# A language-model block with routed experts on one core: first list and third choice moved between a scan and its rotations

## What is computed

```python
h = W.T[x] + b + positions                        # embedding
u = layernorm(h)
Bu = einsum('blh,ph->blp', u, B_bar)              # state-space layer, 64 complex states
xs = associative_scan(x[t] = Lambda_bar * x[t-1] + Bu[t])
h = h + gelu(2 * Re(einsum('blp,hp->blh', xs, C)) + D * u)
x = layernorm(h)
top 2 of 8 experts by logits x @ router_w.T + router_b, weights softmax of the two
out = h + sum over the two: weight * (fc2_e @ (silu(h1) * h2) + fc2_b),  (h1, h2) = fc1_e @ x + fc1_b
```

## Time and profile before

| | us |
|---|---|
| runs (three) | 192.73, 191.54, 193.65 |
| median | 192.73 |
| profiled execution, its own time | 190.8 |
| its span, first to last instruction | 189.0 |
| mean granted TensorE clock | 0.818 of full |
| busy: TensorE, VectorE, ScalarE, GpSimd | 132.8, 112.4, 77.3, 91.0 |
| fourth scan on VectorE starts | 69.70 |
| third scatter on GpSimd, first issue | 77.05 |
| fourth scatter on GpSimd, first issue | 95.47 |

### The profile page before, as it was taken

How to read it: one execution, slowest core, us unless ns; L and a number is a source line. 1 busy time by engine, 2 the same in 40 slices (tenths; PEclk the granted TensorE clock), 3 DMA queues, 4 the chain that set the end, 5 groups by cost and what they waited for, 6 DMA issues and landing times.

```text
span 189.0 us, 3503 instructions
## 1 busy us (share of the span) xinstructions
PE 132.8 (70%) x805; PEld 105.0 (56%) x805; DVE 112.4 (59%) x472; ACT 77.3 (41%) x245; POOL 91.0 (48%) x113
## 2 busy tenths in 40 slices
PE   0273169998869879751991269999996979867910
PEld 0021116758559458541981169988886978765300
DVE  4975159599894896840660027755665665542484
ACT  2223216145182152842542065656555656554000
POOL 5777850000574674573267634645554645446200
PEclk9998555897885975996589559999999999999555
DMA  4222147050151431422133113332310100100297
GB/s 137 69 57 56 47 120 168 3 164 3 27 215 42 129 113 43 101 68 70 45 89 85 55 29 98 102 87 72 100 34 32 36 22 28 42 28 27 75 363 230
DMA packets 15093, 15.65 MB, mean 83 GB/s; under 512 B 2995, under 2 KB 11701, under 8 KB 15074
## 3 DMA queue, kind: packets, MB, share of 16 engines
q1 hardware_dynamic: 10914, 9.39, 18.5%
q0 software_dynamic: 2784, 5.28, 8.8%
q10 hardware_dynamic: 1376, 0.77, 1.3%
HBM read 9.62 MB, written 6.27 MB: 84 GB/s over the span
## 4 chain that ended last, share of the span: by engine, by line
PE 48%; DVE 24%; another core or an unknown queue 10%; issue 9%; ACT 6%; DMA 1%; DVEq 0%; ACTq 0%
PE bank L1238 9%; PE bank L1214 8%; PE bank L1224 8%; PE bank L1204 8%; PE bank L1056 7%; PE bank L1258 3%; DVE stats L626 2%; DVE res L841 1%; DVE zst L613 1%; PE bank L1030 1%; DVE res L624 1%; ACT xT L957 1%; ACT ysb L986 1%; ACT w1b L932 1%
## 5 line engine op out<-in xcount | busy, mean ns | idle before, releaser
L355 POOL DMA_INDIRECT sorted_rows<-rows,slot x32 | 32.2, 1005 | 42.4 <-DVE slot L656 33.8
L753 DVE SCALAR_TENSOR_TENSOR act_h<-bank,w1b,sil 128x128 f32<-128x128 f32 x78 | 23.6, 344 | 33.7 <-ACT sil L966 20.9
L1238 PE MATMUL bank<-w_sb,act_h 128*128 x156 | 26.9, 296 | 11.9 <-ACT ysb L986 10.1
L366 POOL DMA_INDIRECT results<-ysb,dest x22 | 21.7, 985 | 18.3 <-ACT ysb L986 11.6
L1238 PEld LDWEIGHTS bank<-w_sb,act_h 128*128 128x128 f32 x156 | 21.5, 200 | 14.3 <-issue 13.8
L1224 PE MATMUL bank<-xT,w1b 128*128 128x128 f32 x156 | 25.8, 292 | 5.1 <-issue 4.1
L966 ACT ACTIVATE sil<-bank,w1b 128x128 f32<-128x128 f32 x78 | 24.7, 375 | 6.1 <-PE bank L1214 4.4
L1214 PE MATMUL bank<-xT,w1b 128*128 128x128 f32 x156 | 25.7, 290 | 0.0
L366 POOL DMA_INDIRECT results<-ysb,xt x17 | 17.2, 1009 | 17.6 <-ACT ysb L986 15.3
L1224 PEld LDWEIGHTS bank<-xT,w1b 128*128 128x128 f32 x156 | 22.3, 206 | 5.5 <-issue 4.3
L957 ACT COPY xT<-bank 128x128 f32<-128x128 f32 x39 | 10.4, 268 | 33.1 <-PE bank L1204 18.5
(11 more groups left out here) (232 smaller groups left out, 200.2 us busy)
## 6 DMA issues: line engine op xcount, KB each, us to landing
w_sb<-w_all SPq DMA_DIRECT2D x8, 386.0 KB
xt<-sorted_rows SPq DMA_DIRECT2D x39, 65.0 KB, 1.8
yres<-results SPq DMA_DIRECT2D x8, 256.0 KB, 4.0
sorted_rows<-pad SPq DMA_DIRECT2D x1, 520.0 KB, 6.1
sorted_rows<-rows,slot POOLq DMA_INDIRECT x32
out<-res SPq DMA_DIRECT2D x2, 256.0 KB, 3.3
results<-ysb,dest POOLq DMA_INDIRECT x22
results<-ysb,xt POOLq DMA_INDIRECT x17
```

Source lines behind the costliest of these rows:

```text
L355: gp.indirect_dma_start(sorted_rows[:, :], bass.IndirectOffsetOnAxis(ap=slot[:, k, t:t + 1], axis=0), rows[:, k, t, :], None).then_inc(s_s ...
L366: gp.indirect_dma_start(results[:, :], bass.IndirectOffsetOnAxis(ap=target, axis=0), ysb[i][:, :], None, bounds_check=bound, oob_is_err=Fa ...
L753: v.scalar_tensor_tensor(act_h[i % 2][:, q], ps_l[sides(i)][:, q], w1b[i % 4][:, 2 * HID + 2 + c:2 * HID + 3 + c], sil[i % 2][:, q], ALU.a ...
L1238: ins = te.matmul(ps_o[sides(i)][:, 0:D], act_h[i % 2][:, c * P:(c + 1) * P], w_sb[:, bass.ds(at + W1 + c * D, D)], start=(c == 0), stop=( ...
```

## The change

Three calls change places. On VectorE `early_table(0)` and `choose(2)` go from behind `scan(3)` to its inside, behind the scan proper and ahead of the two rotations of group 3. On TensorE `positions(2)` and `count_rows(1)` go from behind the rotated products of group 3 to ahead of them. No instruction is added or removed.

```diff
@@ scan(g), VectorE @@
                 step(v.tensor_tensor_scan(zst[:, :], decay[:, :], zin[:, :], 0.0, ALU.mult, ALU.add))
+                if g == NG - 1:
+                    early_table(0)
+                    choose(2)
                 if g >= 1:
                     dve.wait_ge(s_y, 2 * g)
                 v.tensor_tensor(by_batch(zrot[:, 0, :]), by_batch(zst[:, :]), cos_b, ALU.mult).then_inc(s_zrot, 1)
@@ order on VectorE @@
             scan(3)
-            early_table(0)
-            choose(2)
             find_slots(2)
             early_counts(1)
             add_gelu(3)
@@ order on TensorE @@
             pe.wait_ge(s_rotin, NG)
             idle_products(1, ps_vs)
+            positions(2)
+            count_rows(1)
             rotated(3, 0)
             rotated(3, 1)
-            positions(2)
-            count_rows(1)
             idle_products(3, ps_vs)
             find_ends(1)
```

## The result

The changed kernel took 198.24 us (median of 4 runs, 197.99 to 199.34), the kernel before 192.72 (4 runs, 191.54 to 193.65). The ratio is 1.0301 with a 95% interval of 1.0232 to 1.0369: slower by 5.5 us, where 1.5 us less had been forecast. The profiled execution of the changed kernel took 197.99, with a span of 196.3 against 189.0.

What follows compares the result with a forecast made beforehand. TensorE was taken to bound the change's 4 us stretch and the long pause what follows. The slots' −1.58, with the first tile's 1.40 covered, rounded to −1.5: 192.73 − 1.5 = 191.2 us, range 189.6 to 195.3.

Steps and rivals of the forecast that it cites:

- What bounds, and what ends the pause: ScalarE's 6.00 us pause before copying xnT bounds what follows; it ends 1.45 us after the third scatter's last issue.
- rival a: The pause before xnT's copy has its own length whatever GpSimd does: +1.4, so 194.1 us; chance 0.12.
- an instruction fetch: Possible alternative cause of the pause before xnT: a sequencer stalls for its program block; time 194.1 us, no separate chance.
- Rival (c): The third group's earlier slots are worth nothing and both shifts drown: 192.7 us; chance 0.13.
- The rotations, +2.01: On VectorE, the third group's two rotations come 2.01 us later, behind the list and choice block of 2.10 us.
- a margin of 0.2: At the block's start on VectorE, the list's products were to be ready 0.2 us ahead, so no wait.
- The slots, 1.58 sooner: VectorE's third slots end at 74.66 instead of 76.24, so GpSimd's third scatter starts and ends 1.58 us sooner.
- Positions and count hidden: TensorE's positions and count, an estimated 0.7 us, are hidden to 0.1 behind the wait for the first rotation.
- The first tile +1.40, paid nowhere: First tile's input copy on ScalarE is 1.40 us late (2.01 − 0.61), covered by some 4 us of pause.
- rival (b): The hold on TensorE's signals catches the first tile: +1.4 to +3.8 us, 194.1 to 196.5, middle 194.7; chance 0.25.
- From xnT on everything moves along: After xnT's copy, fourth logits, choice, slots, scatter and the second pause's end all move 1.58 us sooner.
- the 0.7 us that the clock might have given back: TensorE's shorter idle time after the pause might keep its clock high: taken as 0, bounds −0.7 and +0.2.

Runs made afterwards that it cites:

- e12: VectorE half of the change alone, TensorE's order as before, against the kernel before on chip 10 (191.12): 193.09 us, ratio 1.011.
- e11: Changed kernel with SyncE's loads of tiles 3 to 8 held until the third scatter has landed, against the kernel before on chip 10 (191.12): 188.68 us, 0.9879.
- e8: Only third choice and third positions moved ahead, first list and second count left behind, against the kernel before on chip 4 (192.39): 196.31 us, ratio 1.0205.
- e7: Changed kernel with GpSimd's third scatter waiting for the first tile's silu, against the kernel before on chip 4 (192.39): 197.34 us, ratio 1.0321.
- e14: Changed kernel with SyncE's loads of tiles 3 to 8 held until the third scatter has landed, against the kernel before on chip 5: 157.26 us, ratio 1.0215.

## Why the prediction was wrong

**What bounds, and what ends the pause.** Right for the third scatter. The pause ended 1.4 to 1.7 us after its last issue's end in five kernels (after, e12, e11, e8), and 0.25 after it in e7. And with the scatter shifted by 3.7 between two kernels on one chip the copy of xnT shifted by 3.55. Moving the scatter behind the tile moved the pause (e7). The length of its own (rival a) is out: ScalarE stood idle ahead of xnT for 6.00, 5.97, 2.10 and 0.53 us (before, e12, e11, e7). Nor does an instruction fetch end it: no instruction packet moves during the pauses of after, e12, e11 and e8, and in e7 the two that move have done so by 91, while the pause lasts until 93.65. Rival (c), that both shifts drown, is out as well: on chip 10 either shift showed up at xnT.

**The rotations, +2.01.** The term of the sum that was mis-sized. They came 3.83 late. The block took its 2.0, but VectorE waited 1.93 for the list's signal ahead of it, where I had seen that its products would be there and a margin of 0.2. All of it is a late signal, the very thing that I had read from the earlier trace rows and applied to nothing but the expert tiles. The list's last product had ended 0.88 before the scan did. In e14 on chip 5 it lies in the same place after the scan's start, and VectorE goes on without a wait (TensorE's row first, then VectorE's):

```profile
57.71 0.19 PE L1172 MATMUL bank<-owner_a,weight_e 8*1 8x9 f32 x2
...
57.55 1.22 DVE L615 TENSOR_TENSOR_SCAN zst<-decay,zin 128x512 f32<-128x512 f32 x1
58.80 0.16 DVE L698 TENSOR_TENSOR tile_ri<-bank,row_t 1x9 int32<-1x9 f32 x1
```

The waits of 0.43 and 0.44 above are something else: there the product ends 0.3 after the scan. The wait of 1.93 has the same length on chip 4 (e7). Why this signal is late is open. The second scatter is still being issued beside it, its last issue 2.39 after the scan's start, but it is so in e11 and e12 too, where the product ends 1.2 us later and its signal is there at once.

**The slots, 1.58 sooner.** They were 0.22 later after the scan, since the same 1.93 stood ahead of them too. The scatter started at 7.57 after the scan instead of 5.8. The working itself was sound: with the short wait the slots were 1.26 sooner (e11) and 1.25 (e8).

**Positions and count hidden.** Right: over at 74.06, before the rotated products' start at 74.49. Without pauses TensorE's half costs nothing that can be measured: on chips 5 and 7 the VectorE half alone has 1.0116 and 1.0149, the whole change 1.0103. Nearly all is in the VectorE half there, about 1%. With pauses the halves can't be taken apart like this: the VectorE half alone has 1.011 on chip 10 and the whole change 1.0301, and it is TensorE's half that brings the third slots forward (8.73 after the scan without it) and the scatter onto the first tile. The chips differ, though, and so does the wait for the list (0.44 and 1.93).

**The first tile +1.40, paid nowhere.** This is the step that failed. Its transposed input was copied 3.95 later after the scan (80.46 less 68.66, against 77.55 less 69.70), not 1.40: 1.8 more from the rotations, and the 0.61 us of idle that I had counted as taken up was there again (0.74 us). It was never slack: ScalarE was waiting for TensorE's transposition of the tile, which stands behind the rotated products and moved with them in full, from 7.54 to 11.34 after the scan (before, then after). On chip 5 the profile puts the same wait of 0.60 us down to it.

```profile
77.24 0.27 PE L1204 MATMUL bank<-ident,xt 128*128 128x128 f32 x1
```

```profile
80.00 0.42 PE L1205 MATMUL bank<-ident,xt 128*128 128x128 f32 x1
```

The silu came 4.36 late. Then the cover was not there: of the 4 us that I called covered, the pause took them not as slack but cut the tile in two, and everything that TensorE's order has ahead of the fourth logits was done behind the pause. That is rival (b), given 0.25 and up to 3.8 us. Its mechanism is shown: when the scatter is moved behind the tile, the tile passes (e7). Its point was not met as stated. It needed a hold within 5.9 of the scatter's start; the first tile's silu was prompt 6.5 after it and its act_h, due 7.0 after, was held. But it stood close. The first transposition or logits whose signal is seen to be late had ended 5.8 us after the third scatter's start in e11 and in e7, 5.9 in before and e12, 6.2 in e8 and 6.6 in after. Even with rotations and scatter where they were forecast, the third tile's transposition, near 5.9, would have stood at this edge, and in e8, with the rotations at 3.48, act_h, due 6.3 after the start, was held.

**From xnT on everything moves along.** Wrong in size: from xnT (+3.33) to the fourth scatter (+4.96) 1.63 more are lost, since the first tile's second product now stands between, with TensorE at 1.2 GHz, and the second pause gave another 1.8. Rival (b) was priced with the work ahead of xnT only, and the 0.7 us that the clock might have given back went the other way: the granted clock was 0.50 for about 13.7 us after the idle time (87.1 to 100.8), against about 10.2 before (86.0 to 96.3). The idle time behind that bound was also added up wrong: with work 1.40 later and the pause's end 1.58 sooner it is 4.3 − 3.0, so 1.4 us and not 2.

**In sum.** −1.5 as forecast became +5.5. For the forecast's mechanism there is one kernel that had its conditions, the first tile out of the hold and the scatter early: e11, xnT 1.2 sooner and 2.4 us less than before on its chip. It needed a wait that the change does not have.

**Open.** What let the first tile pass in e11: the held loads, the chip, or only its place, since its act_h came 5.8 after the scatter's start where e8's was due 6.3 after. The changed kernel did not run on chip 10, nor held loads on chip 4. That SyncE's loads beside the scatter are part of the cause was thus not shown, and e7 shows that a pause comes without them. Which chip the result ran on is not on record either. What holds the signals is not named by any trace, nor why chips 5 and 7 have none of it.

## What to carry to other kernels

A pause that covers a loss has a beginning as well as an end. Before work is moved towards it, find which signal was the last prompt one, and count what stands behind that signal in every engine's fixed order, for all of it is paid if it is caught. Where one signal is read as held, ask it of every wait of the change that falls beside the same kind of DMA run, also of those whose inputs look ready. And run both kernels on more than one chip, since what a move is worth here was +3%, +1% or, with one more wait, −1.2% by the chip.

## What was unexpected of the hardware

The same kernel takes 153 to 154 us on two chips and 191 to 192 on two others, where, as in the result, VectorE and ScalarE stand still for 4 to 9 us with all inputs computed. Where SyncE's loads and a run of GpSimd's indirect DMAs fall together there, SyncE's steps stretch as well: in the result's changed kernel its register instruction for a tile load takes 37 to 42 ns up to 78.3 and 727 ns at 79.8, the next ones start at 83.4 and 87.7. On chip 5 it stays at 37 to 47 ns throughout.

```profile
L265 SPq FUSED_REGOPS  x9: 3/37/727, 74.0 to 87.7; - x9
...
L754 DVEq EVENT_SEMAPHORE  x2: 49/2351/4653, 83.1 to 91.7; - x2
```

```profile
L265 SPq FUSED_REGOPS  x18: 37/37/47, 63.7 to 91.5; - x18
```

The first are the changed kernel's instructions of one line on SyncE's and VectorE's queues in the result, the last the same kernel's on chip 5 (minimum, median and maximum in ns). The wait's own row, 4653 ns, is thus where such a hold can be seen, before any engine's idle time is put down to a releaser.
